# Decoder layer, change from self- to cross-attention: order of the last four units, earlier statistics, two banks for the last outputs, context split one step sooner

## The reference

```
x = x + self_attention(layernorm(x))        # 32 heads, 8 key/value heads, 512 cached keys + 128 new
x = x + cross_attention(layernorm(x), ctx)  # inside: rmsnorm * ln_weight; 32 heads, mask and position bias
x = x + ffn(layernorm(x))                   # 512 -> 2048 -> 512, gelu

# self-attention, per head:
scores = (q @ k_full.T) / sqrt(128);  attn = softmax(scores);  out = attn @ v_full
result = concat(out) @ wo.T
```

## Time and profile before

| what | value |
|---|---|
| median of three runs | 1938.24 us |
| the profiled execution's own time | 1940.8 us |
| its span, first to last instruction | 1939.0 us |
| PE busy | 1880.7 us (97%) |
| DVE busy | 1353.3 us (70%) |
| ACT, POOL busy | 1030.8 us, 1039.3 us |
| granted TensorE clock, mean | 0.992 of full speed |

### The profile page before, as it was taken

How to read it: one execution, slowest core, us unless ns; L and a number is a source line. 1 busy time by engine, 2 the same in 40 slices (tenths; PEclk the granted TensorE clock), 3 DMA queues, 4 the chain that set the end, 5 groups by cost and what they waited for, 6 DMA issues and landing times.

```text
span 1939.0 us, 31847 instructions
## 1 busy us (share of the span) xinstructions
PE 1880.7 (97%) x9902; PEld 1601.3 (83%) x9902; DVE 1353.3 (70%) x2177; ACT 1030.8 (53%) x2265; POOL 1039.3 (54%) x832
## 2 busy tenths in 40 slices
PE   8899999999999999998999999999999999999998
PEld 6788888888888888876888888888888888888887
DVE  7688888888888888867666666666666666667132
ACT  3566666666666666655444444444444444446444
POOL 3677777777777777772433433333344344324643
PEclk9899999999999999998999999999999999999999
DMA  7544444445544444551222222222222222212232
GB/s 250 126 122 121 123 124 119 121 122 124 124 121 122 122 121 122 152 141 44 90 84 73 84 89 83 67 74 84 89 78 89 82 73 84 79 44 87 91 117 80
DMA packets 142283, 201.04 MB, mean 104 GB/s; under 512 B 29715, under 2 KB 67219, under 8 KB 141715
## 3 DMA queue, kind: packets, MB, share of 16 engines
q1 hardware_dynamic: 142226, 200.33, 36.9%
HBM read 98.25 MB, written 18.09 MB: 60 GB/s over the span
## 4 chain that ended last, share of the span: by engine, by line
PE 79%; DVE 11%; issue 5%; ACT 3%; SPq 1%; POOL 0%; DMA 0%; DVEq 0%; ACTq 0%
PE bank L1376 22%; PE bank L1377 21%; PE bank L1378 21%; PE bank L1456 7%; DVE negmax L997 4%; PE bank L1599 2%; DVE xacc L1016 2%; PE bank L1600 2%; PE bank L1646 2%; PE bank L1647 2%; DVE probT L1005 1%; ACT prob L643 1%; DVE oT_lo L1010 1%; SPq L295 1%; ACT V_hi L584 0%
## 5 line engine op out<-in xcount | busy, mean ns | idle before, releaser
L490 POOL TENSOR_TENSOR pT_lo<-pT_lo,pT_hi 128x512 fp32r<-128x512 f32 x320 | 406.8, 1293 | 192.0 <-ACT pT_hi L584 192.0
L1016 DVE SCALAR_TENSOR_TENSOR xacc<-bank,rinv,xacc 128x512 f32<-128x512 f32 x504 | 362.5, 730 | 4.5 <-PE bank L1378 4.5
L643 ACT ACTIVATE prob<-bank,negmax 128x640 f32<-128x640 f32 x256 | 203.7, 796 | 275.0 <-DVE negmax L997 274.6
L1005 DVE STREAM_TRANSPOSE probT<-prob 128x640 f32<-128x640 f32 x256 | 214.3, 837 | 81.5 <-ACT prob L643 81.3
L997 DVE TENSOR_REDUCE negmax<-bank 128x1 f32<-128x640 f32 x256 | 206.8, 808 | 24.8 <-PE bank L1456 18.6
L584 ACT ACTIVATE pT_hi<-pT_lo 128x512 fp32r<-128x512 f32 x320 | 185.7, 622 | 6.1 <-DMA pT_lo<-probT 5.9
L473 POOL TENSOR_TENSOR xwo_lo<-xwo_raw,xwo_hi 128x512 fp32r<-128x512 f32 x32 | 41.3, 1291 | 273.0 <-ACT xwo_hi L584 273.0
L473 POOL TENSOR_TENSOR xwq_lo<-xwq_raw,xwq_hi 128x512 fp32r<-128x512 f32 x32 | 41.4, 1293 | 246.6 <-ACT xwq_hi L584 246.6
L1376 PE MATMUL bank<-wx_hi,cT_hi 128*128 128x256 f32 x512 | 143.0, 279 | 1.1 <-DVE xk L1125 1.1
L1378 PE MATMUL bank<-wx_hi,cT_lo 128*128 128x256 f32 x512 | 142.5, 278 | 0.0
L1377 PE MATMUL bank<-wx_lo,cT_hi 128*128 128x256 f32 x512 | 142.5, 278 | 0.0
(11 more groups left out here) (200 smaller groups left out, 5523.3 us busy)
## 6 DMA issues: line engine op xcount, KB each, us to landing
pT_lo<-probT SPq DMA_DIRECT2D x1024, 80.0 KB, 2.1
w_raw<-in_w SPq DMA_DIRECT2D x64, 256.0 KB, 2.8
xturned<-xturn SPq DMA_DIRECT2D x61, 256.0 KB, 2.0
xpraw<-xturned SPq DMA_DIRECT2D x244, 64.0 KB, 2.0
wx_raw<-in_wq SPq DMA_DIRECT2D x32, 256.0 KB, 2.7
wo_raw<-in_wo SPq DMA_DIRECT2D x32, 256.0 KB, 2.7
wx_raw<-in_xwv SPq DMA_DIRECT2D x16, 512.0 KB, 4.1
xwk_raw<-in_xwk SPq DMA_DIRECT2D x32, 256.0 KB, 2.8
```

The source lines that it names most:

```text
L490: g.tensor_tensor(tile, tile.bitcast(F32), four(pT_hi[:, j, :]), ALU.subtract).then_inc(a["pTlo"], 1)
L643: s.activation(prob[:, i % 2, :].rearrange("p (a t) -> p a t", a=2), S_bank[i % 2], ACT.Exp, bias=negmax[:, u % 2, i:i + 1], scale=1.0, ac ...
L1005: v.transpose(probT[:, u % 2, :, :, i * 32:(i + 1) * 32], prob[:, i % 2, :].rearrange("p (t j n) -> p j t n", j=4, n=32)).then_inc(a["turn ...
L1016: v.scalar_tensor_tensor(xacc[:, 4 * half + i, :], M, rinv[:, k, i:i + 1], xacc[:, 4 * half + i, :], ALU.mult, ALU.add).then_inc(sems["y"], 1)
```

## The change

- **Order of the last four units.** Units 60, 61, 62 and 63 become (head 30, half 0), (head 31, half 0), (head 30, half 1), (head 31, half 1). The function `unit_of` and its table were there (the cross-attention uses it); now queries, outputs and adds of the self-attention use it too. Half 0 is complete with unit 61, count 248.
- **Statistics.** `ln_stats(0)` and `second_variance(0)` move up in DVE's list, between the last add of unit 61 and the first of unit 62. `second_inner(0)` comes behind the adds of unit 62, `out_lo(64)` (the low part for unit 63) between `second_inner(0)` and `second_outer(0)`.
- **Banks.** The last four outputs use banks 0, 1, 0, 1; half 0 is transposed into banks 4, 2, 7 and 3. PE no longer waits for all adds ahead of these transposes.
- **Context.** Splits of the four chunks move from steps 59 to 62 to steps 58 to 61 on ACT and POOL, and the value weights from step 62 to 61. Loads of chunks 2 and 3 move up a step; those of chunks 0 and 1 and of the value weights stay where they are.
- **PE** runs `values(0, 0)` before the outputs of unit 61. **ACT** splits the first weights later (`c_weights`), behind the first square root and behind the first keys.

The diff, without a block in which the unchanged function `second_variance` leaves its old place:

```diff
@@ -200,7 +200,7 @@
         W_bank = [bank[:, 4 + i, :] for i in range(2)]
-        W_last = [bank[:, i, :] for i in (0, 1, 2, 4)]
+        W_last = [bank[:, i, :] for i in (0, 1, 0, 1)]
         O_bank, M_bank = bank[:, 6, :], bank[:, 7, :]
@@ -218,7 +218,7 @@
-        LN2_bank = [[bank[:, i, :] for i in banks] for banks in ((0, 1, 2, 3), (2, 3, 7, 6))]
+        LN2_bank = [[bank[:, i, :] for i in banks] for banks in ((4, 2, 7, 3), (2, 3, 7, 6))]
         V_first = [bank[:, i, :] for i in (7, 3, 6, 5)]
@@ -316,8 +316,8 @@
                     sp.dma_start(xwv_raw[:, :, :], xwv[0]).then_inc(s_xvraw, 16)
-                if UNITS - 4 <= n < UNITS - 2:
-                    ch = n - (UNITS - 6)
+                if UNITS - 5 <= n < UNITS - 3:
+                    ch = n - (UNITS - 7)
                     sp.wait_ge(s_clo, ch - 1)
@@ -495,8 +495,8 @@
                     rotate_wq(h + 3, 1 - hp, (it * 2 + (u // 2 + 1) // 2 + 2) * 16)
-                if static and UNITS - 5 <= n < UNITS - 1:
-                    ch = n - (UNITS - 5)
+                if static and UNITS - 6 <= n < UNITS - 2:
+                    ch = n - (UNITS - 6)
                     split_lo(cT_lo[:, ch, :], c_raw[:, ch % 2, :], cT_hi[:, ch, :], s_chi, ch, s_clo)
@@ -506,7 +506,7 @@
                 a_step(7, u)
-                if u == 6:
+                if u == 5:
                     split_lo(xwv_lo[:, :, :], xwv_raw[:, :, :], xwv_hi[:, :, :], c["vwhi"], 0, c["vwlo"])
@@ -729,13 +729,11 @@
                 a_step(7, u)
-                if u == 6:
+                if u == 5:
                     raw_split(xwv_hi[:, :, :], xwv_raw[:, :, :], s_xvraw, 16, c["vwhi"])
-            for h_ in range(2):
+            def c_weights(h_):
                 raw_split(xwk_hi[:, h_], xwk_raw[:, h_], s_xraw["k"][h_], 16, c["kwhi"])
                 raw_split(xwq_hi[:, h_], xwq_raw[:, h_], s_xraw["q"][h_], 16, c["qwhi"])
-                if h_ == 0:
-                    out_hi(UNITS - 1)
@@ -767,10 +765,13 @@
             ln_sqrt(2, 1)
+            c_weights(0)
             v_evac(0, 1, 2, V_first[1])
+            out_hi(UNITS - 1)
             ln_sqrt(2, 2)
...
             k_evac(0, 0, 1)
+            c_weights(1)
             act.wait_ge(s_lnw, 16 * C)
@@ -1015,6 +1016,13 @@
                                        xacc[:, 4 * half + i, :], ALU.mult, ALU.add).then_inc(sems["y"], 1)
+
+            def second_variance(half):
+                for b in range(4 * half, 4 * half + 4):
+                    last = v.bn_aggr(meanvar[:, b, :], stats[:, b, :])
+                link(last)
+                sl = slice(4 * half, 4 * half + 4)
+                v.tensor_scalar(nrm[:, 0, sl], meanvar[:, sl, 1], EPS, None, ALU.add).then_inc(L[2, "stat"], 1)
@@ -1053,7 +1061,8 @@
-                    accumulate(a, n - m, (u + 4 - m) % 4, (u - m) % 2, j, W_bank[j % 2], None)
+                    half = unit_of(n - m)[1] if static else (u - m) % 2
+                    accumulate(a, n - m, (u + 4 - m) % 4, half, j, W_bank[j % 2], None)
@@ -1065,6 +1074,10 @@
                     add(3, 3)
+                if static and n == UNITS:
+                    dve.wait_ge(a["y"], LAST1 - 8)
+                    ln_stats(0)
+                    second_variance(0)
                 if here:
@@ -1102,10 +1115,7 @@
             for i in (2, 3):
-                accumulate(a, UNITS - 2, (UNITS - 2) % 4, UNITS % 2, i, W_bank[i % 2], None)
-            dve.wait_ge(a["y"], LAST1 - 4)
-            ln_stats(0)
-            out_lo(UNITS)
+                accumulate(a, UNITS - 2, (UNITS - 2) % 4, 1, i, W_bank[i % 2], None)
@@ -1157,11 +1160,11 @@
-            second_variance(0)
+            second_inner(0)
             v_evac(0, 0, 1, V_first[0])
-            second_inner(0)
+            out_lo(UNITS)
+            second_outer(0)
             v_evac(0, 1, 2, V_first[1])
-            second_outer(0)
             last_attention(range(4))
@@ -1525,11 +1528,13 @@
                     if more2:
-                        queries(n + 2, h + 1, ((u + 2) // 2) % 2, k, chunks)
+                        h2, half2 = unit_of(n + 2) if static else (h + 1, k)
+                        queries(n + 2, h2, h2 % 2 if static else ((u + 2) // 2) % 2, half2, chunks)
...
                     if outs:
-                        head_out(n - 2, h - 1, ((u - 2) // 2) % 2, j, W_bank[j % 2])
+                        h0 = unit_of(n - 2)[0] if static else h - 1
+                        head_out(n - 2, h0, h0 % 2 if static else ((u - 2) // 2) % 2, j, W_bank[j % 2])
@@ -1601,24 +1606,24 @@
             n = UNITS - 1
-            for i in range(4):
-                head_out(n - 2, (n - 2) // 2, ((n - 2) // 2) % 2, i, W_bank[i % 2])
             pe.wait_ge(s_clo, C)
             pe.wait_ge(c["vwlo"], 1)
+            pe.wait_ge(a["qlo"], UNITS)
             values(0, 0, None, V_first[0])
+            for i in range(4):
+                head_out(n - 2, NH - 1, 1, i, W_bank[i % 2])
             for j in range(KT):
...
             for i in range(4):
-                head_out(n - 1, (n - 1) // 2, ((n - 1) // 2) % 2, i, W_bank[i % 2])
+                head_out(n - 1, NH - 2, 0, i, W_bank[i % 2])
             for j in range(KT):
...
             for i in range(4):
-                head_out(n, n // 2, (n // 2) % 2, i, W_last[i])
-            pe.wait_ge(a["y"], LAST1)
+                head_out(n, NH - 1, 1, i, W_last[i])
             pe.wait_ge(c["vlo"], 2)
```

More of the change, by code:

```diff
@@ L1126, in xk_lo_evac @@
                                 ALU.subtract).then_inc(c["klo"], 1)
-            def second_variance(half):
-                for b in range(4 * half, 4 * half + 4):
-                    last = v.bn_aggr(meanvar[:, b, :], stats[:, b, :])
-                link(last)
-                sl = slice(4 * half, 4 * half + 4)
-                v.tensor_scalar(nrm[:, 0, sl], meanvar[:, sl, 1], EPS, None, ALU.add).then_inc(L[2, "stat"], 1)
             def second_inner(half):
```

## The result

| | median | runs | ratio to before (95% interval) |
|---|---|---|---|
| before | 1939.01 us | 20 (1936.45 to 1942.61) | |
| changed | 1942.68 us | 20 (1937.68 to 1945.08) | 1.0016 (1.0009 to 1.0023) |

The forecast of 0.8 us more was 2.3 us too low. The two medians differ by 3.7 us; 1942.68 lies inside the range of 1935.0 to 1943.0, 0.3 us under its top.

What follows compares the result with a forecast made beforehand. PE, busy 97% of the span, was taken as the bound, so only its idle time and slow clock could be won. +4.3 - 5.2 = -0.9 us, plus 1.7 for the clock, gave +0.8: 1939.0 us, range 1935.0 to 1943.0.

Steps and rivals of the forecast that it cites:

- Chunk 0, +4.3: Step 58: ACT waits for the first context chunk's load, delaying POOL's tiles and the pv of unit 58 by 4.3 us.
- The rival of a hidden wait: Wait for chunk 0 costs nothing because ACT idles anyway; total about 1934 us; chance 0.11.
- End of step 61, +2.4: POOL makes cT_lo and wx_lo ahead of unit 61's tiles, so PE's pv of unit 61 starts 2.4 us later.
- DVE ahead of unit 62's third output: Moved statistics and variance delay unit 62's first add; PE gets 1.5 us of new idle time, 2.3 in one piece.
- Refinement held by POOL: Half 0's refinement: three DVE instructions wait for POOL's tiles and splits, 0.3 + 1.2 + 1.2 us, ending at 880.7 instead of 878.3.
- The rival that it is not held: POOL does not hold up half 0's refinement; total 1.6 us better, 1937.4 us; chance 0.09.
- Second transposes, -0.9: Half 1's transposes: 5.2 us gained there against 4.3 lost in step 59, so 0.9 us sooner at an unchanged clock.
- the gain is smaller: Half-1 statistics, variance and xk_lo stay ahead of xT_lo; one more POOL collision adds 1.2 us; 1940.2 us; chance 0.13.
- Clock, +1.7: Around the new PE gaps: one more short fall to half speed than before, 3.4 us long, costing 1.7 us.
- the slow clock stays: Slow stretches follow the gaps in steps 59 and 62, costing up to 5 us each; total +5.8, 1944.0 us; chance 0.17.
- three signs of being wrong: First cT_hi without idle time; first_queries(0) under 3 or over 8 us sooner against step 62's end; half speed over 10 us.

Runs made afterwards that it cites:

- e12: Changed kernel with dummy matmuls, results overwritten, filling PE's gaps in step 59, step 62 and at unit 62's third output, ending inside them; ratio to before 0.9999.
- e2: Kernel before with only the context part of the change (earlier splits and loads, first values ahead of unit 61's outputs); ratio to before 1.0041.
- e3: Changed kernel with the load of context chunk 0 issued ahead of step 58's transposing DMAs instead of behind them; ratio to before 0.9984.
- e4: Changed kernel with the value weights split inside step 61 (ACT before its last exponential, POOL behind the tiles); ratio to before 0.9990.
- e5: Changed kernel with half 0's statistics and variance moved behind the first two adds of unit 62 in DVE's list; ratio to before 1.0022.
- e10: Changed kernel with POOL waiting for the half-0 refinement before xwk_lo; one run, 113.02 us from step 58's last common idle time to the second transposes.
- e1: Changed kernel with its context part undone (splits, loads and first values placed as in the kernel before); ratio to before 0.9974.
- e7: Changed kernel with the edits of e3 and e4 together; ratio to before 0.9970.

## Why the prediction was right, and where it was off

Its steps can be held against e12, which is the change at a full clock. Instants in us from the anchor; the forecast's are its own numbers with the 4.3 us of step 59 added and 796.20 taken off, the others starts of PE's rows, but for the refinement, which is DVE's end of it:

| step | before | forecast | e12 | changed |
|---|---|---|---|---|
| `pv` of unit 58 | 13.25 | 17.5 | 17.51 | 18.42 |
| `pv` of unit 61 | 52.05 | 58.7 | 58.63 | 61.60 |
| unit 62's third output | 76.56 | 82.4 | 82.48 | 87.24 |
| half 0 refined | | 88.8 | 88.80 | 93.71 |
| unit 63's third output | 90.45 | 93.0 | 92.72 | 98.16 |
| second transposes | 107.92 | 107.05 | 107.71 | 112.97 |

- **Chunk 0, +4.3.** Right: +4.26 at the `pv` of unit 58 in e12. In the changed kernel's own profile the landing took 5.5 us instead of 4.5 and made it +5.17. The rival of a hidden wait is out: e2 has the gap with the context part alone, and e3 removes it by the load alone.
- **End of step 61, +2.4.** Right: 58.63 - 52.05 = 6.58, less 4.26, is 2.3; e4 gives it back.
- **DVE ahead of unit 62's third output.** Right to 0.1 us. But the 1.5 us of new idle time there were no loss in the end: in e5 they are gone, and PE waits them out further on.
- **Refinement held by POOL.** Right: three of its instructions took 0.43, 1.21 and 1.22 us in e12, and the variance ahead of them 0.90. In the changed kernel two took 0.69 and 1.20, and the variance 0.46. The rival that it is not held is out, and e10 gives no sign that its 1.6 us would have come through.
- **Second transposes, -0.9.** -0.2 in e12. 0.9 us were lost between unit 63's third output and the second transposes, where the prediction gave an instant (898.95) without the rows behind it. Nearly all of it is one instruction, the variance of half 1, held by POOL's mask. DVE, then POOL in e12, and DVE in the kernel before:

```profile
891.53 1.03 DVE L1025 TENSOR_SCALAR nrm<-meanvar 128x4 f32<-128x4 f32 x1
```

```profile
891.49 1.05 POOL L516 TENSOR_SCALAR negmask<-mask_sb 128x1024 f32<-128x1024 uint8 x1
```

```profile
893.32 0.17 DVE L1134 TENSOR_SCALAR nrm<-meanvar 128x4 f32<-128x4 f32 x1
```

It took 1.03 instead of 0.17 us, and both end at 892.5; in the changed kernel it took 0.84. This is the collision with the mask that the rival "the gain is smaller" had named and priced at 1.2. No run takes it away by itself.

- **Clock, +1.7.** This is the step that failed, by size. "I take one such fall more than before" stood for 1.7 us on top of a sum from which the 10.2 us fall of before was already gone. Three falls came, 17.0 us at half speed, and they cost 4.4 us by e12: from row to row of the table 2.1, 1.8 and 0.7 us. The rival "the slow clock stays" (+5.8 in all, from 9.6 us at half speed on) had the places right, behind the split gap and in step 62, though each lasts 6.8 us instead of 10.2. The reason I gave against it, that dense work follows, is refuted by the stretch 854 to 860: 5.89 of 6.00 us busy, at 0.53. The price was off the other way, half a microsecond for each slow one. 3.8 us of the slow clock lie ahead of the `pv` of units 58 and 61, where PE waits for POOL in any case; and about 1.5 us of what it then loses shorten PE's later waits for DVE (1.95 instead of some 2.5 us at unit 62's third output, 0.15 instead of 1.04 at unit 63's).

So the time fell into the range in part by luck. Of the three signs of being wrong that the prediction gave, one came: more than 10 us at half speed. At its own price 17.0 us would have cost 8.5, and -0.9 + 8.5 is +7.6, outside the range; that each slow microsecond cost half of that kept the time inside. The errors in chunk 0's landing, the mask and the clock all lie on one side.

The sum with measured terms: -0.2 at a full clock, +4.4 for the clock and +0.85 for the landing are +5.05, as the trace has it. By the ratio it is 3.1 us (1.7 to 4.5). The profile after had one landing a microsecond late, and how many falls an execution has varies (before's 2.5 us gap went without a fall in its profile, e1's equal gap had one of 3.4). That may be why the 20 executions give less than this one profile; it is not shown. How often each fall comes in unprofiled runs stays open.

## What to carry to other kernels

A load that an engine awaits delays all that stands behind it in that engine's list, so move its issue up by as much as its first use. Work moved to the end of a pipeline step stands ahead of the next step's first tile, and PE pays for the whole chain (3.00 us); inside the step, where ACT and POOL had slack, it cost PE nothing (0.70 us in e4, 0.71 before the change). And where PE is the bound, price each new gap as the gap plus the slow clock behind it (here 2.1 us behind 3.14 + 0.94, 1.8 behind 3.00 and 0.7 behind 1.95), and measure that by keeping PE busy in the gap with work that is thrown away and ends inside it: this separates the two.

## What the runs showed that I had not expected

- Gaps of 2.2 and 1.6 us with 0.7 us of work between (e2), and of 3.0 us (changed, e2, e3), were each followed by 3.4 or 6.8 us at 1.2 GHz, also where PE was busy throughout behind them. Shorter ones went either way: 2.5 us was followed by none before and by 3.4 in e1 and e7; 1.95 us by 3.4 in the changed kernel, and 1.96 us by none in e3.
- Adding matmuls made a kernel whose PE is busy for 97% of the span faster: PE busy went from 1880.0 to 1883.4 us, and the ratio from 1.0016 to 0.9999.
- The same 512 KB load took 4.5 us from issue to landing in the profile of before and 5.5 in that of the changed kernel, and with ACT waiting for it that is PE time one for one: 0.85 us more on ACT (changed against e12), and the `pv` of unit 58 0.91 us later.
